# A four-layer cross-attention kernel: the high and low parts of the softmax maxima move from VectorE to GpSimd

## The reference

```python
def _attend(q, k, v):
    attn = jnp.einsum('bhnd,bhsd->bhns', q, k) * SCALE
    attn = jax.nn.softmax(attn, axis=-1)
    o = jnp.einsum('bhns,bhsd->bhnd', attn, v)
    ...
x = x + _attend(q, k, v) @ ca_proj_w + ca_proj_b
xm = _ln(x) * (1.0 + sc_ff) + sh_ff
h = jax.nn.gelu(xm @ fc1_w + fc1_b, approximate=True)
x = x + g_ff * (h @ fc2_w + fc2_b)
```

## Time and profile before

| | us |
|---|---|
| median of 3 runs | 5098.0 (5096.28 to 5099.81) |
| the profiled execution | 5102.48 |
| its span, first to last instruction | 5100.7 |
| PE busy, of the span | 4603.9 |
| VectorE busy | 4093.3 |
| ScalarE busy | 3563.0 |
| GpSimd busy | 1629.2 |

### The profile page before, as it was taken

The page is one execution under the profiler, slowest core; times in us unless marked ns, Lnnn a source line. Parts: engine busy times, 40 slices in busy tenths (PEclk is TensorE's granted clock), DMA queues, the critical chain, the costliest instruction groups (busy, mean ns, idle before and its releaser), DMA issues.

```text
span 5100.7 us, 122448 instructions
## 1 busy us (share of the span) xinstructions
PE 4603.9 (90%) x47748; PEld 2159.2 (42%) x47748; DVE 4093.3 (80%) x8590; ACT 3563.0 (70%) x4867; POOL 1629.2 (32%) x2319
## 2 busy tenths in 40 slices
PE   5799999999998788868999999999999999999997
PEld 2344444444443577753333343443434443333333
DVE  5799999999886444428889989999998988888885
ACT  2387787787777344434777878777777777777776
POOL 4344444444431011022333342433223232323321
PEclk9799999999999899987999999999999999999999
DMA  2212212212111111121212122121212212212110
GB/s 67 70 53 59 65 52 69 62 49 70 49 46 37 61 55 56 57 55 42 66 46 73 52 70 58 51 72 46 72 56 57 64 44 61 57 45 66 37 56 8
DMA packets 347979, 284.41 MB, mean 56 GB/s; under 512 B 52775, under 2 KB 303866, under 8 KB 347404
## 3 DMA queue, kind: packets, MB, share of 16 engines
q1 hardware_dynamic: 339048, 273.29, 18.9%
q10 hardware_dynamic: 8356, 3.29, 0.3%
HBM read 86.98 MB, written 26.11 MB: 22 GB/s over the span
## 4 chain that ended last, share of the span: by engine, by line
PE 39%; DVE 7%; ACT 5%; issue 4%; ACTq 1%; POOL 0%; DMA 0%; DVEq 0%; POOLq 0%; SPq 0%
PE pb_obank L1155 14%; PE pb_dbank L1168 9%; PE pb_aunit L1131 6%; DVE pb_c_maxs L846 6%; ACT pb_probs L946 4%; PE pb_aunit L1215 2%; PE pb_aunit L1205 1%; PE pb_dbank L1230 1%; DVE pb_c_mbf L856 1%; PE pb_aunit L1256 1%; PE pb_aunit L1250 1%; PE pb_aunit L1240 1%; PE pb_aunit L1194 1%; PE pb_aunit L1139 1%; ACTq L939 1%
## 5 line engine op out<-in xcount | busy, mean ns | idle before, releaser
L846 DVE TENSOR_REDUCE pb_c_maxs<-pb_dbank 128x1 f32<-128x512 f32 (+1 forms) x3584 | 2043.3, 627 | 308.2 <-PE pb_dbank L1168 292.4
L946 ACT ACTIVATE pb_probs<-pb_aunit 128x1024 f32<-128x1024 f32 (+1 forms) x1792 | 1750.5, 1025 | 268.6 <-PE pb_aunit L1131 213.6
L846 DVE TENSOR_REDUCE pa_c_maxs<-pa_dbank 128x1 f32<-128x512 f32 (+1 forms) x1792 | 1023.8, 626 | 129.5 <-PE pa_dbank L1168 118.2
L946 ACT ACTIVATE pa_probs<-pa_aunit 128x1024 f32<-128x1024 f32 (+1 forms) x960 | 937.9, 1024 | 178.5 <-PE pa_aunit L1131 155.6
L1155 PE MATMUL pb_obank<-pb_probs,kept_vaug 128*9 128x256 f32 x13312 | 948.1, 382 | 1.8 <-ACT pb_probs L946 0.4
L1168 PE MATMUL pb_dbank<-kept_kst,kept_qst 62*128 62x512 bf16 (+1 forms) x4096 | 763.3, 341 | 63.2 <-DVE pb_c_maxs L846 54.5
L1131 PE MATMUL pb_aunit<-kept_qst,kept_kst 64*128 64x256 bf16 x6144 | 575.9, 273 | 103.9 <-ACT pb_probs L946 69.7
L1168 PEld LDWEIGHTS pb_dbank<-kept_kst,kept_qst 62*128 62x128 bf16 x4096 | 234.4, 93 | 587.4 <-DVE pb_c_maxs L846 416.1
L1155 PE MATMUL pa_obank<-pa_probs,kept_vaug 128*9 128x256 f32 x6656 | 468.2, 381 | 1.0 <-ACT pa_probs L946 0.6
L1168 PE MATMUL pa_dbank<-kept_kst,kept_qst 62*128 62x512 bf16 (+1 forms) x2048 | 394.7, 343 | 18.8 <-DVE pa_c_maxs L846 14.0
L1131 PEld LDWEIGHTS pb_aunit<-kept_qst,kept_kst 64*128 64x128 bf16 x6144 | 233.7, 95 | 400.7 <-ACT pb_probs L946 167.9
(11 more groups left out here) (522 smaller groups left out, 6182.8 us busy)
## 6 DMA issues: line engine op xcount, KB each, us to landing
kept_kst<-kept_keys SPq DMA_DIRECT2D x576, 200.1 KB
kept_cin<-in_ctx SPq DMA_DIRECT2D x37, 768.0 KB
context_turned<-moe_ct SPq DMA_DIRECT2D x16, 800.5 KB, 3.6
kept_qst<-pb_c_qsp SPq DMA_DIRECT2D x360, 32.0 KB
kept_turned<-context_turned SPq DMA_DIRECT2D x16, 400.5 KB
kept_turned<-context_turned SPq DMA_DIRECT2D x16, 400.0 KB
pa_z_kst<-pa_z_ksp SPq DMA_DIRECT2D x192, 32.0 KB
pb_z_qst<-pb_z_qsp SPq DMA_DIRECT2D x192, 32.0 KB
```

The lines of the kernel that those rows point to most:

```text
L846: dve.tensor_reduce(dst, dbank[N % RING_D][:, 0:cnt * width].rearrange("p (s c) -> p s c", s=cnt), AX.X, ALU.max).then_inc(d_free, 1)
L946: act.activation(probs[u % RING_P][0:rows].rearrange("p a i q -> p (a i q)"), src[0:rows, :], ACT.Exp, scale=HD ** -0.5).then_inc(a_free, 1)
```

## The change

The three instructions behind the reduction leave VectorE's program and stand in GpSimd's, under the same token `Rn`, with the same operands. VectorE keeps L851 alone, and its wait for `m_hl` ahead of it. GpSimd waits for `m_neg` (the reduction), as VectorE did, for the transposes of the item before, and between the two steps for `m_bf`. The list `PROG` and its table of costs stay as they are, and so do PE, ScalarE and SP.

```diff
                     wait(dve, s.m_hl, 2 * (2 * i + half - 1))
                     dve.tensor_reduce(s.negm[half][:].rearrange("p t a b -> p (t a b)"), s.maxs[:, half].rearrange("p t a b c -> p (t a b) c"), AX.X, ALU.max,
                                       negate=True).then_inc(s.m_neg, 1)
-                    dve.wait_ge(s.m_neg, 2 * i + half + 1)
-                    if i:
-                        dve.wait_ge(a_full, a_done(("Rt", half), s, i - 1))
-                    dve.tensor_copy(s.mbf[half][:], s.negm[half][:]).then_inc(s.m_bf, 1)
-                    dve.wait_ge(s.m_bf, 2 * i + half + 1)
-                    dve.tensor_copy(s.mhl[half][:, :, :, 0, :], s.mbf[half][:]).then_inc(s.m_hl, 1)
-                    dve.tensor_tensor(s.mhl[half][:, :, :, 1, :], s.negm[half][:], s.mbf[half][:], ALU.subtract).then_inc(s.m_hl, 1)
...
         @block.gpsimd
...
-                if k == "ln":
+                if k == "Rn":
+                    half = tok[1]
+                    pool.wait_ge(s.m_neg, 2 * i + half + 1)
+                    if i:
+                        pool.wait_ge(a_full, a_done(("Rt", half), s, i - 1))
+                    pool.tensor_copy(s.mbf[half][:], s.negm[half][:]).then_inc(s.m_bf, 1)
+                    pool.wait_ge(s.m_bf, 2 * i + half + 1)
+                    pool.tensor_copy(s.mhl[half][:, :, :, 0, :], s.mbf[half][:]).then_inc(s.m_hl, 1)
+                    pool.tensor_tensor(s.mhl[half][:, :, :, 1, :], s.negm[half][:], s.mbf[half][:], ALU.subtract).then_inc(s.m_hl, 1)
+                elif k == "ln":
```

## The result

The changed kernel takes 5228.3 us (median of 4 runs, 5223.1 to 5229.5) beside 5098.9 us before: the ratio is 1.0248, with a 95% interval of 1.0236 to 1.0261. The forecast was 5221 us. The profiled execution has a span of 5226.6 us, 125.9 us more than before.

What follows compares the result with a forecast made beforehand. PE, busy 90% of the span, was taken as the bound. Terms 116 + 2 + 30 - 15 - 10 = 123 us on the profiled 5102.5 us gave 5225; the runs' median lies 4.5 us lower, so 5221 us, range 5161 to 5273.

Steps and rivals of the forecast that it cites:

- The queue behind gelu_cube: At the second-half maxima of 30 items, PE waits for the moved step queued behind GpSimd's gelu_cube: 116 us more.
- The step's length on GpSimd: The three moved instructions take 0.78 us together on GpSimd, between 0.76 and 1.36 us.
- What is given back: Behind each of 30 stands, rested ScalarE and VectorE make PE's small waits vanish: 0.5 us each, 15 us in all.
- The clock: PE's gaps of 3 to 5 us mostly cost a stretch at the lower clock: 1.0 us each, 30 us.
- Rival (1): PE stands at the transposes as forecast, but the clock stays up: 5191 us, chance 0.23.
- What VectorE's relief gives: The lighter VectorE shortens PE's waits for the maxima: a gain of 10 us, bounds 0 and 74.
- (2): Faster: the port between VectorE and GpSimd mattered, PE's 74 us of waits go: 5024 us at best, chance 0.07.
- (3): Slower: the step costs 1.4 us or more on GpSimd, PE stands longer: 5258 us, up to 5273, chance 0.13.
- the marks that were named: VectorE's busy time falls about 180 us, PE's transposes show 30 long waits for GpSimd, second-phase clock falls below 1.00.

Runs made afterwards that it cites:

- e5: Kernel before, nothing moved; at the same 30 transposes PE also waits until GpSimd's gelu_cube of the item before has ended: 5223.8 us, ratio 1.0246.
- e1: Changed kernel, but in the 30 items where gelu_cube stood ahead, GpSimd makes the high and low parts before gelu_cube: 5076.1 us, ratio 0.9955.
- e3: Changed kernel, but only the 30 executions behind gelu_cube are on GpSimd, the other 130 stay on VectorE: 5258.2 us, ratio 1.0314.
- e4: Changed kernel, with PE making 19 or 28 unread identity transposes ahead of its wait in the same 30 items: 5186.5 us, ratio 1.0169.
- e7: Kernel before, nothing moved; in the second phase GpSimd's last k0 instruction waits for VectorE's first-half parts: 5066.1 us, ratio 0.9933.

## Why the prediction was right, step by step

The direction, the place, the mechanism and the size were right. That the time was only 7 us off is luck in part: three terms were wrong, and their errors cancelled.

**The queue behind gelu_cube** was the deciding term and was right. It was put at 116 us more than before; the 30 stands of the changed kernel are 15 x 4.37 + 46.8 = 112 us, of which PE stood some 5 already. e5 makes the loss without moving anything, e1 takes it away by the order alone. The single stands were 3.7 and 4.7 us in the forecast and are 3.04 and 4.37. In the second phase most of the difference is the step's length: from the end of L682 to the end of L1048 are 0.58 us, where 0.08 + 0.78 were taken. In the first phase the layer norm ahead of gelu_cube also ends sooner, by the 0.4 us that e3 shows.

**The step's length on GpSimd** was taken as 0.78 us and is 0.63 from the first start to the last end. The 0.2 us for each instruction were right: the casts take 196 ns and the subtraction 217. The gaps of 0.08 us that were added hardly show, as the three lengths make 0.61 of the 0.63. The GPSIMD Engine Reference of the Trainium skill (section 4.1, Engine selection) has some 2 times VectorE's time for two inputs and roughly line rate for one input; the forecast's estimate by it, 1.0 us, doubled all three instructions, though two of them are casts with one input. The trace has 1.4 times for the subtraction (217 beside 160 ns) and 1.1 for the casts (196 beside 174), so less than the 2 times at this size. A cast of 256 elements takes 396 ns, so 0.8 ns an element; by that estimate some 0.18 us of the 0.196 at 16 elements do not depend on their number.

**What is given back** was put at 15 us and is 0. This step failed. e4 against e1 shows it: the items differ by the stand to within 0.02 us, so nothing behind it runs faster. As I read it, PE's small waits behind the place are not waits for late work but come from its own order and the two banks of the ring, and return after each stand as they were; that cause is argued, no run tests it.

**The clock** was put at 30 us and cost 42. In the changed kernel it fell at every one of the 30 stands, where the forecast let some go free. Rival (1), that the clock stays up, is out: without the fall the time is 5186 us, e4, close to the 5191 that it would have had.

**What VectorE's relief gives** was put at 10 us and is 23 (5098.9 - 5076.1, e1; the 5 us that PE stood for L859 in the first phase are among them). In layer 2 the forecast's argument held mostly: the wait moves from L1168 to L1178, and 0.33 us an item is left. In layer 3 GpSimd is done with k0 earlier against PE (in the trace of before L1085 ends at 4515.36, 1.7 us ahead of the transposes at 4517.05; in layer 2 at 3476.30, 1.0 us ahead of 3477.31), and 0.98 us an item is won, which the forecast left out by working out only an item of layer 2. In the first phase it is 0.70 us. The two rows of layer 3:

```profile
4513.36 2.00 POOL L1085 TENSOR_TENSOR kept_keys<-kept_keys 128x1024 bf16<-128x1024 f32 x1
4517.05 0.39 PE L1176 MATMUL pb_aunit<-kept_ident,pb_c_mhl 128*16 128x128 f32 x2
```

So the account is 112 + 42 - 23 = 131 us, against 129 measured, where the forecast had 116 + 2 + 30 - 15 - 10 = 123.

**The rivals.** (2), faster by the port, needed stands under 2.5 us an item, and they are 3.04 and 4.37. What it builds on is there: GpSimd's instructions do hold VectorE's up, and e7 wins 34.5 us by keeping the two apart, but the stands outweigh that in the change as it is. (3), a slower step, is out: the step was shorter. Of the marks that were named, VectorE's busy time fell by 155 us, not by 180: the 181 us were summed by line, and in the trace these instructions overlap each other and their neighbours (all three lines together cover 167 us). The rows for L1178 appeared, with 30 long waits among their 48. The clock fell.

## What to carry to other kernels

When a step moves to an idler engine, its price is what stands ahead of it in that engine's order, not how busy the engine is (here 32%): look at what the engine is doing when the step's input is ready and when its reader comes. Where PE was the path, as here, a wait of PE cost its full length, and a long one also the work at half clock behind it. And where two engines hold each other up on a small instruction, putting the long one behind the short one was enough here (e7); nothing had to move.

## What the hardware showed that was not expected

- The granted clock fell for all 30 stands of 3.0 to 4.8 us, at 1.4 us of time each; waits of about 0.9 us at the same line, in layer 2, left it at 2.4 GHz. The length alone doesn't decide in between: two stands of 2.5 us left it up (e5), and a gap of 1.56 us was followed by a fall. Transposes that nobody reads hold it up (e4).
- GpSimd starts an instruction slightly before the end that the profile gives to the one ahead: L1045 at 4652.52, L682 until 4652.57.
- A VectorE instruction of 0.17 us that runs beside a GpSimd instruction of 2 us can take nearly as long as that one (1979 ns, in 15 of 64 before); with that one held back no such time is left (e7).
